# Decoder on one core: the first tile's running sums ahead of its last projection, row statistics elsewhere in the turn

## The chip, the core and the metric

The kernel runs on one core of one Trainium2 chip. The core has five engines with a queue of instructions each: TensorE (PE) multiplies matrices into eight PSUM banks, VectorE (DVE), ScalarE (ACT) and GpSimd (POOL) work elementwise, and SyncE (SP) only issues DMAs. Each queue runs in its own order; the engines meet at semaphores. The metric is device time in microseconds (us) of one execution. Before the change it is 1161.15 us, the median of three runs (1160.86 to 1164.18).

## The reference

The input is 4 sequences of 512 rows with 512 numbers each, seen as 16 tiles of 128 rows. Six blocks follow one another: a state-space mixer, a read from a memory, a routed feed-forward block, a grouped attention, a second memory read in fp8, and a feed-forward block with rounded weights. The change touches the mixer alone, `mamba3_forward` on `_layernorm(x)`:

```python
u_n = layer_norm(u, ln_w, ln_b)
proj = jnp.einsum('bsd,ed->bse', u_n, in_proj_w)   # z 1024, x 1024, B 128, C 128, dt 16
B = rms_norm(B, bnorm_w);  C = rms_norm(C, cnorm_w)
dA = softplus(dt + dt_bias) * -jnp.exp(A_log)
y = ssd_chunked(x, dA, B, C, CHUNK)   # pairs within a chunk decay by exp(differences of running sums of dA),
                                      # earlier chunks come in through a state
y = y + x * D[None, None, :, None]
y = y * jax.nn.silu(z_flat)
return u + jnp.einsum('bse,de->bsd', y, out_proj_w)
```

## The kernel before

The mixer works tile by tile, with chunks of 128 rows. The order is written out by hand, once for each engine (`tensor_program`, `vector_program`, `scalar_program`, `gpsimd_program`). A prologue takes tile 0 through its projections. Then a loop over i = 1 to 17, called turns here, overlaps three tiles: tile i is projected ("new"), tile m = i-1 gets its decays, products and gate ("mix"), and tile k = i-2 is turned, multiplied by the output weights and added to x ("old"). Four tiles are a sequence; its last hands on no state.

What the change and the prediction speak of, with the lines of `before`:

- **Running sums.** `decay_logs(i)` on POOL (L2063 to L2076) makes the logarithms of tile i's decays and lays them out in the tile `cum`; `running(i)` on PE (L455) sums them down the rows with one matmul; `high_cum` on ACT (L1608) and `low_cum` on DVE (L891) split the sums in a high and a low half; `shape_cum` on ACT (L1618, L1622) puts signs on them; four `spread_cum` on DVE (L901) spread them over heads into `cum_h`. `decay(m, q)` on PE (L469) multiplies these, for tile m in turn m+1, `exp_decay` on ACT (L1632) takes the exponential, `weigh_pair` on DVE (L909) multiplies it with the pair products.
- **Gate.** `project(i, 3)` and `project(i, 4)` on PE (L403) make z; `tanh_z(i, n)` on ACT (L1594) and `gate_z(i, n)` on DVE (L942) turn it into its gate; `gate_y(m, n)` on DVE (L934, L937) uses it.
- **Skip term.** `skip_y(m)` on POOL (L2115) writes x times D into the tile `y`. In turn 1 it waits until `low_piece(5)` on DVE (L852) has taken a piece of the output weights, since `y` lies where a later piece lands. `weigh_xs(m)` (L2133) multiplies `xs` for the state once `y_product` (L488) is through; `state_product` (L499) waits for it.
- **Row statistics.** `a_stats(g)` on DVE (four L819, four L823) takes mean and variance of the four tiles of a sequence; `stats(g)` on POOL makes scales of them one turn later. It comes in turns 1, 5 and 9, for the tiles 4 to 7, 8 to 11 and 12 to 15. `normal(i+1)` on DVE (L831) opens turn i; `turn_un` on PE (L411), `scale_x` on ACT (L1551) and all later work of tile i+1 wait for it.
- **Banks.** `Banks.claim` hands out PSUM banks when the program is built, from a table of expected times and in the order of the claims; a claim waits until the bank's last content has been read.

## Time and profile before

| what | value |
|---|---|
| median of 3 runs | 1161.15 us |
| the profiled execution | 1161.08 us, its span 1159.4 us |
| PE, DVE, ACT, POOL busy | 1044.8, 855.3, 606.0, 464.5 us (90, 74, 52, 40% of the span) |
| chain that ended last | PE 48%, DVE 21%, POOL 14%, issue 9%, ACT 5%, DMA 1% |
| mean granted TensorE clock | 0.967 of full speed |

The span runs from the first to the last instruction of the profiled execution; 1.7 us lie around it. PE is busy for nine tenths of it, but a busy share is a mean: the mixer fills the first 470 us, and in its first 75 us PE stands idle several times. The chain that ended last is followed back from the last instruction, at each step to what released it; a shorter time must shorten this chain.

### The profile page before, as it was taken

To read this page: it belongs to the slowest core of one execution; us is meant where nothing else is said; L and a number is where in the kernel's file an instruction comes from. 1 tells how busy PE (TensorE), PEld (TensorE's weight loads), DVE (VectorE), ACT (ScalarE), POOL (GpSimd) and SP (SyncE) were. 2 spreads that over 40 slices of the span, in tenths; PEclk is the share of its full clock that TensorE was granted. 3 is DMA by queue.
4 is the path that set the end of the run, shared out by engine and by line. 5 is a ranking of instruction groups with operands and counts; after the bars stand their busy time and mean duration, and the time that the engine had idled before them with its cause. 6 is when DMAs were issued, how large, how long until landed. Compare 5 with 4: busy or idle time off the path is not lost.

```text
span 1159.4 us, 14674 instructions
## 1 busy us (share of the span) xinstructions
PE 1044.8 (90%) x4830; PEld 746.7 (64%) x4830; DVE 855.3 (74%) x1615; ACT 606.0 (52%) x1201; POOL 464.5 (40%) x727
## 2 busy tenths in 40 slices
PE   5789999999999999879999689997788999899796
PEld 3667887888778888644545377765556666666342
DVE  5677766776677666726776658776779999989974
ACT  4634444444434443135556547553457877777662
POOL 5344324332433233325778214113544544535420
PEclk9899999999999999989999889998889999999899
DMA  8200000000000000063010044500001112111123
GB/s 297 86 1 1 1 1 1 1 1 1 1 1 1 1 1 6 32 254 118 29 37 1 1 162 147 193 24 1 1 5 22 40 29 52 27 37 43 31 54 87
DMA packets 48427, 52.92 MB, mean 46 GB/s; under 512 B 34528, under 2 KB 35552, under 8 KB 46048
## 3 DMA queue, kind: packets, MB, share of 16 engines
q1 hardware_dynamic: 48352, 51.99, 14.0%
q8 instruction: 39, 0.64, 0.2%
q14 instruction: 36, 0.29, 0.1%
HBM read 39.92 MB, written 4.19 MB: 38 GB/s over the span
## 4 chain that ended last, share of the span: by engine, by line
PE 48%; DVE 21%; POOL 14%; issue 9%; ACT 5%; DMA 1%; DVEq 0%; POOLq 0%; ACTq 0%
PE bank L403 37%; PE bank L488 3%; PE bank L411 3%; DVE cum_h L901 2%; POOL pv L2323 2%; PE bank L479 1%; POOL wq L2239 1%; DVE at L1359 1%; DVE o L1389 1%; POOL wq L2243 1%; PE bank L469 1%; POOL wq L2249 1%; DVE fm L1472 1%; DVE half_lo L1235 1%; POOL wq L2232 1%
## 5 line engine op out<-in xcount | busy, mean ns | idle before, releaser
L403 PE MATMUL bank<-win_hi,a_uT_hi 128*128 128x512 f32 (+1 forms) x320 | 130.1, 407 | 7.3 <-DVE win_lo L852 4.0
L403 PE MATMUL bank<-win_lo,a_uT_hi 128*128 128x512 f32 (+1 forms) x320 | 122.3, 382 | 0.0
L403 PE MATMUL bank<-win_hi,a_uT_lo 128*128 128x512 f32 (+1 forms) x320 | 122.0, 381 | 0.0
L2125 POOL TENSOR_TENSOR y<-y,off 128x512 f32<-128x512 f32 x24 | 37.8, 1573 | 113.8 <-DVE off L922 113.8
L1603 ACT ACTIVATE ex<-bank 128x48 f32<-128x48 f32 x16 | 3.3, 209 | 150.8 <-PE bank L447 150.8
L403 PEld LDWEIGHTS bank<-win_hi,a_uT_hi 128*128 128x128 f32 x320 | 62.5, 195 | 22.0 <-issue 6.4
L403 PEld LDWEIGHTS bank<-win_lo,a_uT_hi 128*128 128x128 f32 x320 | 62.6, 196 | 13.4 <-issue 2.9
L403 PEld LDWEIGHTS bank<-win_hi,a_uT_lo 128*128 128x128 f32 x320 | 62.1, 194 | 11.9
L403 PE MATMUL bank<-wq,eT 128*128 128x512 f32 x128 | 63.5, 643 | 4.9 <-ACT eT L1897 4.6
L488 PEld LDWEIGHTS bank<-xs,wgt 128*128 128x128 f32 x512 | 61.2, 192 | 6.8 <-issue 5.7
L403 PE MATMUL bank<-f,fqT_next 128*128 128x512 fp8e4 (+1 forms) x312 | 64.0, 362 | 1.3 <-DMA fqT_next<-fq 1.3
L488 PE MATMUL bank<-xs,wgt 128*128 128x64 f32 x512 | 61.0, 272 | 0.4 <-DVE wgt L909 0.4
L909 DVE SCALAR_TENSOR_TENSOR wgt<-wgt,cb 128x512 f32<-128x512 f32 x64 | 54.1, 845 | 8.6 <-ACT wgt L1632 8.4
L403 PE MATMUL bank<-wq,b_uT 128*128 128x512 f32 x128 | 59.7, 611 | 0.7 <-issue 0.7
L901 DVE TENSOR_TENSOR cum_h<-cum,eye_h 64x512 fp32r<-64x512 f32 x64 | 59.6, 970 | 1.0 <-ACT cum L1622 0.5
L403 PE MATMUL bank<-ctx,pT 128*128 128x512 f32 x128 | 58.2, 598 | 0.0
L1594 ACT ACTIVATE zs<-bank 128x512 f32<-128x512 f32 x32 | 18.8, 588 | 67.8 <-PE bank L403 67.8
L2050 POOL TENSOR_SCALAR sq<-sq 128x2 f32<-128x2 f32 x16 | 3.1, 191 | 127.2 <-ACT cs L1568 127.1
L403 PE MATMUL bank<-wout_hi,yT_hi 128*128 128x512 f32 x128 | 51.9, 406 | 1.6 <-DVE yT_lo L974 1.6
L403 PEld LDWEIGHTS bank<-f,fqT_next 128*128 128x128 bf16 x312 | 29.6, 98 | 34.6 <-issue 4.5
L403 PE MATMUL bank<-wout_lo,yT_hi 128*128 128x512 f32 x128 | 50.5, 394 | 0.0
L403 PE MATMUL bank<-wout_hi,yT_lo 128*128 128x512 f32 x128 | 50.4, 394 | 0.0
(335 smaller groups left out, 3046.1 us busy)
## 6 DMA issues: line engine op xcount, KB each, us to landing
wchunk<-w_in SPq DMA_DIRECT2D x32, 256.0 KB, 5.0
stage<-f_in SPq DMA_DIRECT2D x4, 1408.0 KB, 5.9
x<-x_in SPq DMA_DIRECT2D x16, 256.0 KB, 6.0
land<-win_in SPq DMA_DIRECT2D x4, 1024.0 KB, 7.6
wq<-ctxT_in SPq DMA_DIRECT2D x4, 1024.0 KB, 8.3
ctx<-ctx_in SPq DMA_DIRECT2D x4, 1024.0 KB, 5.7
out<-x SPq DMA_DIRECT2D x16, 256.0 KB, 2.7
first_stage<-f_in SPq DMA_DIRECT2D x2, 1408.0 KB, 14.2
```

What stands on the lines that cost most here:

```text
L403: made = e.matmul(bank, a, b, start=start and n == 0, stop=stop and n == len(pairs) - 1)
L411: made = e.transpose(bank[:, k * P:(k + 1) * P], src[:, k * P:(k + 1) * P], idn[:])
L469: e.matmul(bank[:], cum_s[q // 2][rows, :], cum_h[q][rows].rearrange("p a b -> p (a b)"), start=True, stop=True).then_inc(sig("decay_summe ...
L479: e.matmul(bank[:], cT[:], state[:, n * 512:(n + 1) * 512], start=True, stop=True).then_inc(sig("off_done"), 1)
L488: made = e.matmul(bank[:, j * HD:(j + 1) * HD], wgt[h // HG][:, h % HG, :], xs[m % 2][:, h * HD:(h + 1) * HD], start=True, stop=True)
L901: e.tensor_tensor(cum_h[q][rows], cum[rows, :].bitcast(F32).unsqueeze(1).broadcast_to([P // 2, HG, P]), eye_h[rows, first:first + HG].unsq ...
L909: e.scalar_tensor_tensor(out=wgt[q][:], in0=wgt[q][:], scalar=1.0, in1=cb[:].unsqueeze(1).broadcast_to([P, HG, P]), op0=ALU.min, op1=ALU.m ...
L1235: e.tensor_tensor(half_lo[m][f % 2][:], wchunk[m][f % WCHUNKS][:], half_hi[m][f % 2][:].bitcast(F32), ALU.subtract).then_inc(sig(f"half_lo ...
L1359: e.tensor_reduce(raw, prod[:, 0:s + 1, :].rearrange("p t (h d) -> p (t h) d", d=AHD), AX.X, ALU.add).then_inc(sig("at_step"), 1)
L1594: e.activation(zs[i % 2][:, n * 512:(n + 1) * 512], banks.of["proj_z", i, 3 + n][:], ACT.Tanh, scale=0.5).then_inc(sig("z_tanh"), 1)
L2125: e.tensor_tensor(y[m % 2][:, cols], y[m % 2][:, cols], off[:], ALU.add).then_inc(sig("y_off"), 1)
L2323: e.tensor_tensor(grouped(pv[turn % 2][:]), shared(n - n % BATCH + t, (R + 1) * AHD), weights(n, t), ALU.mult).then_inc(sig("pv_ready"), 1)
```

## The change

Nothing is computed otherwise. Four edits move work:

1. On PE, `running(0)` comes ahead of `project(0, 4)`. On ACT, `high_cum(0)` and `shape_cum(0)` come ahead of the tile's two or one last steps (`tanh_z(0, 0)`, `tanh_z(0, 1)`, `scale_x(1)`).
2. On DVE, `low_cum(0)` comes ahead of `gate_z(0, 0)`, the four spreads of tile 0 move from turn 1 into the prologue, and `gate_z(0, 1)` from the prologue into turn 1, behind `turned_bc(0)`.
3. On POOL, in turn 1 alone, `skip_y(0)` comes behind `decay_logs(1)`.
4. On DVE, `a_stats` moves in turns 1, 5 and 9 from behind the last two spreads to ahead of `gate_z(i, 1)`.

```diff
@@ tensor_program
             turn_un(1)
+            running(0)
             project(0, 4)
-            running(0)
@@ vector_program
             e.tensor_tensor(bcw[:], bw[:], cw[:], ALU.mult).then_inc(sig("mixer_consts"), 1)
+            low_cum(0)
             gate_z(0, 0)
-            gate_z(0, 1)
-            low_cum(0)
+            for q in range(NG):
+                spread_cum(0, q)
@@ vector_program, in the loop
                 if mix:
                     turned_bc(m)
                 if i == 1:
-                    for q in range(NG):
-                        spread_cum(0, q)
+                    gate_z(0, 1)
@@
                 if old:
                     low_yT(k, 1)
+                if i + 3 < NT and (i + 3) % TPB == 0:
+                    a_stats((i + 3) // TPB + 1)
                 if new:
                     gate_z(i, 1)
@@
                 if new:
                     spread_cum(i, 2)
                     spread_cum(i, 3)
-                if i + 3 < NT and (i + 3) % TPB == 0:
-                    a_stats((i + 3) // TPB + 1)
@@ scalar_program
             scale_x(0)
+            high_cum(0)
             tanh_z(0, 0)
+            shape_cum(0)
             tanh_z(0, 1)
             scale_x(1)
-            high_cum(0)
-            shape_cum(0)
@@ gpsimd_program
                     root_bc(i)
-                if mix:
+                if mix and i > 1:
                     skip_y(m)
                 if new:
                     decay_logs(i)
+                if i == 1:
+                    skip_y(m)
```

VectorE at the end of the prologue and the start of turn 1, - before and + now (`zs` is the gate, `un` the normalised tile, `cb` and `cT` the turned B and C):

```order
-L942 SCALAR_TENSOR_TENSOR zs_111<-zs_111,bank 128x512 x2
-L891 TENSOR_TENSOR cum<-bank,cum 32x128 x2
+L891 TENSOR_TENSOR cum<-bank,cum 32x128 x2
+L942 SCALAR_TENSOR_TENSOR zs_111<-zs_111,bank 128x512
+L901 TENSOR_TENSOR cum_h_115<-cum,eye_h 64x512
+L901 TENSOR_TENSOR cum_h_116<-cum,eye_h 64x512
+L901 TENSOR_TENSOR cum_h_117<-cum,eye_h 64x512
+L901 TENSOR_TENSOR cum_h_118<-cum,eye_h 64x512
 L831 TENSOR_SCALAR un<-x_51,a_mv_88,a_rs_90 128x512
 L878 COPY cb<-bank 128x128
 L880 TENSOR_SCALAR cT<-bank,bcw 128x128
```

The low half and the four spreads now stand ahead of the normalisation of tile 2, and one of the two gate steps stands behind `cT`, where the spreads had been.

VectorE at the end of turn 5, before the change (`yT_lo` and `y` belong to the tiles k and m, `a_st` and `a_mv` are the statistics of the next rows):

```order
L974 TENSOR_TENSOR yT_lo<-bank,yT_hi 128x512
L942 SCALAR_TENSOR_TENSOR zs_112<-zs_112,bank 128x512
L901 TENSOR_TENSOR cum_h_115<-cum,eye_h 64x512
L901 TENSOR_TENSOR cum_h_116<-cum,eye_h 64x512
L934 TENSOR_TENSOR y_123<-y_123,bank 128x512
L937 TENSOR_TENSOR y_123<-y_123,zs_111 128x512
L901 TENSOR_TENSOR cum_h_117<-cum,eye_h 64x512
L901 TENSOR_TENSOR cum_h_118<-cum,eye_h 64x512
L819 BN_STATS a_st<-x_57 128x6
...
L823 BN_AGGR a_mv_88<-a_st 128x2 x4
L980 SCALAR_TENSOR_TENSOR x_52,b_sum<-bank,x_52 128x512
```

The same place in the changed kernel:

```order
L974 TENSOR_TENSOR yT_lo<-bank,yT_hi 128x512
L819 BN_STATS a_st<-x_57 128x6
...
L823 BN_AGGR a_mv_88<-a_st 128x2 x4
L942 SCALAR_TENSOR_TENSOR zs_112<-zs_112,bank 128x512
L901 TENSOR_TENSOR cum_h_115<-cum,eye_h 64x512
L901 TENSOR_TENSOR cum_h_116<-cum,eye_h 64x512
L934 TENSOR_TENSOR y_123<-y_123,bank 128x512
L937 TENSOR_TENSOR y_123<-y_123,zs_111 128x512
L901 TENSOR_TENSOR cum_h_117<-cum,eye_h 64x512
L901 TENSOR_TENSOR cum_h_118<-cum,eye_h 64x512
L980 SCALAR_TENSOR_TENSOR x_52,b_sum<-bank,x_52 128x512
```

The eight statistics instructions stand ahead of the gate step instead of ahead of the addition to x; turns 1 and 9 read alike.

GpSimd in turn 1, before (`sq` are the norms of B and C, `dt` the logarithms of tile 1):

```order
L2050 TENSOR_SCALAR sq_101<-sq_101 128x2
L2052 TENSOR_TENSOR sq_101<-sq_101,mhalf 128x2
L2115 TENSOR_TENSOR y_123<-xs_109,dvec 128x1024
L2063 TENSOR_SCALAR dt_103<-dt_103 128x16
L2065 TENSOR_TENSOR dt_103<-dt_103 128x16
L2068 TENSOR_TENSOR dt_103<-dt_103,nega 128x16
L2070 CAST cum<-dt_103 128x4x8
L2072 TENSOR_TENSOR cum<-dt_103,cum 128x4x8
L2076 TENSOR_SCALAR cum<-cum 128x8x8
L2133 TENSOR_TENSOR xs_109<-xs_109,ex_113 128x1024
```

Now L2115 stands behind L2076 and ahead of L2133; nothing else moves there.

## Rows read from the trace of the kernel before

**Rows 1.** Granted clock by stretches: busy us and counts of the engines, PEclk, DMA share, GB/s.

```profile
31.30:36.00 4.70, 4.67 (x11) 3.70 (x12) 2.16 (x3) 1.53 (x2) 2.61 (x4) 0.50 0.86 318
42.80:46.20 3.40, 3.40 (x9) 2.59 (x9) 1.43 (x7) 3.10 (x11) 0.92 (x2) 0.51 0.01 2
190.00:192.00 2.00, 2.00 (x10) 1.90 (x9) 0.17 (x1) 1.71 (x9) 0.70 (x2) 0.50 0.04 8
```

**Rows 2.** Instructions of PE in order of time: start, us, what, [idle before, releaser].

```profile
31.33 0.80 PE L403 MATMUL bank<-win_hi,a_uT_hi 128*128 128x512 f32 x1 [4.02 <-DVE win_lo L852]
...
38.58 0.38 PE L447 MATMUL bank<-dt,ones 128*128 128x16 f32 x2
41.16 0.48 PE L469 MATMUL bank<-cum_h,cum_s 67*128 67x512 f32 x1 [2.21 <-DVE cum_h L901]
...
57.95 0.30 PE L455 MATMUL bank<-upto_r,cum 128*128 128x128 f32 x1 [3.13 <-POOL cum L2076]
...
66.57 3.57 PE L499 MATMUL bank<-xs,bs 128*128 128x512 f32 x4 [3.73 <-POOL xs L2133]
...
74.91 0.63 PE L411 MATMUL bank<-ident,un 128*128 128x128 f32 x4 [2.07 <-DVE un L831]
```

**Rows 3.** ACT in order of time, end of the prologue.

```profile
38.78 0.99 ACT L1618 ACTIVATE cum_s<-cum,signs 64x128 fp32r<-64x128 f32 x2 [0.74 <-DVE cum L891]
...
40.20 0.19 ACT L1603 ACTIVATE ex<-bank 128x48 f32<-128x48 f32 x1
```

**Rows 4.** POOL in order of time, prologue and turn 1.

```profile
28.89 0.25 POOL L2076 TENSOR_SCALAR cum<-cum 128x64 fp32r<-128x64 f32 x1
...
30.42 3.68 POOL L2105 CAST cum_h<-off 3x512 fp32r<-3x512 f32 x4
...
52.91 2.22 POOL L2115 TENSOR_TENSOR y<-xs,dvec 128x1024 f32<-128x1024 f32 x1 [7.86 <-DVE wout_lo L852]
...
57.56 0.25 POOL L2076 TENSOR_SCALAR cum<-cum 128x64 fp32r<-128x64 f32 x1
63.02 3.40 POOL L2133 TENSOR_TENSOR xs<-xs,ex 128x1024 f32<-128x1024 f32 x1 [5.22 <-PE bank L488]
```

**Rows 5.** DVE in order of time, turns 1 and 2.

```profile
40.33 2.61 DVE L901 TENSOR_TENSOR cum_h<-cum,eye_h 64x512 fp32r<-64x512 f32 x4 [0.51 <-ACT cum L1622]
...
58.60 0.59 DVE L891 TENSOR_TENSOR cum<-bank,cum 32x128 fp32r<-32x128 f32 x2 [0.26 <-ACT cum L1608]
61.78 0.69 DVE L942 SCALAR_TENSOR_TENSOR zs<-zs,bank 128x512 f32<-128x512 f32 x1 [2.59 <-ACT zs L1594]
...
64.59 2.98 DVE L901 TENSOR_TENSOR cum_h<-cum,eye_h 64x512 fp32r<-64x512 f32 x2
...
68.93 1.29 DVE L901 TENSOR_TENSOR cum_h<-cum,eye_h 64x512 fp32r<-64x512 f32 x2
70.25 2.47 DVE L819 BATCH_NORM_STATS2 a_st<-x 128x6 f32<-128x512 f32 x4
...
73.05 1.26 DVE L969 COPY state<-bank 128x512 f32<-128x512 f32 x2
74.23 0.54 DVE L831 TENSOR_SCALAR un<-x,a_mv,a_rs 128x512 f32<-128x512 f32 x1
```

**Rows 6.** DVE in order of time, turns 5 and 6.

```profile
178.02 0.69 DVE L942 SCALAR_TENSOR_TENSOR zs<-zs,bank 128x512 f32<-128x512 f32 x1 [1.35 <-ACT zs L1594]
178.63 2.85 DVE L901 TENSOR_TENSOR cum_h<-cum,eye_h 64x512 fp32r<-64x512 f32 x2
...
188.75 0.54 DVE L831 TENSOR_SCALAR un<-x,a_mv,a_rs 128x512 f32<-128x512 f32 x1
```

**Rows 7.** PE in order of time, starts of turns 6, 10 and 11.

```profile
189.43 0.90 PE L411 MATMUL bank<-ident,un 128*128 128x128 f32 x4 [1.20 <-DVE un L831]
...
304.06 0.63 PE L411 MATMUL bank<-ident,un 128*128 128x128 f32 x4 [1.20 <-DVE un L831]
...
334.26 0.63 PE L411 MATMUL bank<-ident,un 128*128 128x128 f32 x4 [0.82 <-DVE un L831]
```

## The prediction

> **What bounds the kernel now.** I read the chain that ended last first. Between 37 and 75 us it hardly touches PE: it goes over the split and shaping of tile 0's running sums, ACT's exponentials, `skip_y(0)` and `decay_logs(1)` on POOL, one projection on PE, then DVE's whole tail of turn 1 with `a_stats` in it. From turn 3 on it is mostly PE, except at the ends of the turns 5 and 9, where it goes through `a_stats` again. The instructions of PE in order of time give the holes: 4.02 us before `project(0, 4)`, 2.21 us before `decay(0, 0)` behind the spreads, 3.13 us before `running(1)` behind `decay_logs(1)`, 3.73 us before the state product behind `weigh_xs(0)`, and 2.07 us before tile 3's turning behind `normal(3)` [rows 2]; later 1.20 us in each of turns 6 and 10, and 0.82 us in turn 11 [rows 7]. All these lie in the mixer, whose first turn fills slowly. The blocks behind it start when its last tiles are through and their loads wait for those too, so I let every us gained in the mixer pass to the end.
>
> I follow one chain, from tile 0's sums to `normal(3)`, and then the two later places. In front of each step I ask which of its waits ends last.
>
> **Edit 1 and 2, the first tile's sums.** `running(0)` needs `decay_logs(0)`, which ends at 28.89 + 0.25 = 29.14 us [rows 4]. PE is idle until 31.33 [rows 2], so the matmul of some 0.3 us costs nothing there; the margin before it would hold up `project(0, 4)`, now queued behind it, is 2.2 us. The split follows on ACT and DVE, which both wait for `project(0, 4)` in that time. What ends last for `shape_cum(0)` is not the split but POOL's constant rows in `cum_h`, at 30.42 + 3.68 = 34.10 [rows 4]. The shaping takes from 38.78 to DVE's start at 40.33, 1.55 us [rows 3, 5]: the spreads start near 35.7 and end 2.61 us later at 38.3, where they ended at 42.94 before.
>
> That is 4.6 us on the spreads, but the next steps have other waits. `decay(0, 0)` goes right behind the sums, which end at 38.96 [rows 2], so 2.2 us earlier. ACT's exponential of the sums started at 40.20 because it queued behind the shaping [rows 3]; now it waits for the same 38.96 and starts at 39.0. From there ACT works through `scale_x(2)`, two pieces of output weights, two table loads and `exp_decay(0, 1)` with no idle that matters, so this chain gains only 40.20 - 39.00 = **1.2 us**. `normal(2)` is ready at 38.9 and hides in it. The gate step moved into turn 1 costs 0.69 us of DVE [rows 5] between `cT` and the wait for ACT's squares, which is longer. The second projection of turn 1 has its bank from this gate, and starts about 1 us behind `decay(0, 0)` as before, so 2 us earlier. It ends long before `weigh_pair(0, 1)`, which is what `y_product` waits for. So PE gets its time back and uses it for waiting.
>
> **Edit 3, POOL.** `skip_y(0)` started at 52.91, 7.86 us idle behind a weight piece, and `decay_logs(1)` behind it ended at 57.81; `running(1)` waited 3.13 us [rows 4, 2]. Now `decay_logs(1)` runs as soon as ACT's logarithm is there, inside those 7.86 us, and `running(1)` goes right behind `decay(0, 3)`, around 53.5. `skip_y(0)` still waits for the piece (at 52.7 - 1.2 = 51.5) and is still ready for the first `gate_y`. The 4.4 us gained on PE do not reach the end as such: DVE takes `low_cum(1)` only when the weighing and gating before it are through, which had started at 58.60 after 0.26 us idle [rows 5]. It now starts at 58.60 - 1.2 - 0.26 = 57.15. But the second `y_product` is no longer behind a late projection: it follows the last weighing (57.15), ends near 58.1, and `weigh_xs(0)` starts at 58.2 instead of 63.02.
>
> **Edit 4 in turn 1.** `low_cum(1)` ends at 57.75, and DVE used to wait 2.59 us from there for the tanh [rows 5]. `a_stats(2)` takes 73.05 - 70.25 = 2.80 us [rows 5] and fills it: the gate step starts at 60.55 instead of 61.78, still 1.2 us early. Then two things go. The first pair of spreads took 2.98 us and the second, the same work, 1.29 [rows 5]; the first ran against `weigh_xs(0)`, itself 3.40 us long (63.02 to 66.42), because the two excluded each other [rows 4, 5]. With `weigh_xs(0)` at 58.2 to 60.1 they don't meet: **1.7 us**. And `a_stats` is gone from the tail: **2.8 us**. `normal(3)` starts at 74.23 - 1.2 - 1.7 - 2.8 = 68.5; the state product, at 60 to 64, and everything else it needs are there. Start: **-5.7 us**.
>
> `a_stats` itself now runs beside `weigh_xs(0)`. No row shows such a pair. From below its cost is 0; from above one excludes the other, by the 1.7 us of the nearest rows (L901 against L2133). I take 0: of the DVE rows beside long POOL ones, those with one input in SBUF kept their length, those with two did not. The Trainium skill, "SBUF — State Buffer", section Who interferes with whom, says that a DVE instruction with at most one SBUF input and outside the two-port modes does not contend with GpSimd, and one with two does against a GpSimd read. By that rule the cost is 0 too; the first pair of spreads, two inputs, agrees.
>
> Turn 2 keeps its shape behind `normal(3)`: squares, norms, `skip_y(1)`, `stats(2)` and `add_off` on POOL set its pace, each as long as before. PE may run slower there (see the third rival); its slack I estimate at 2 us, 0.8 from the wait that comes a turn later (as in turn 11 [rows 7]) and 1.2 from POOL's chain being the later one of the two that `low_cum(2)` waits for,.
>
> **Edit 4 in turns 5 and 9.** DVE stood idle 1.35 us before the gate step at 178.02 [rows 6]. `a_stats` starts there at 176.67 and ends at 179.47, so gate and spreads begin 1.45 us later. The spreads took 2.85 us against `weigh_xs(4)`, which ends at 180.3; now they begin at 180.1 and take about 1.5. So `gate_y(4, 1)` is 0.1 to 0.3 us late, and the tail without `a_stats` puts `normal(7)` at 188.75 - 2.8 + 0.3 = 186.3. PE wants it at 189.43 - 1.20 = 188.2 [rows 7]: the whole wait of 1.20 us goes, and 1.1 us of the gain lies idle. ACT's `scale_x(7)` and `exp_decay(5, 0)` follow the sums instead of `normal(7)`, 1.2 to 1.3 us earlier, and with them POOL's `stats(3)` chain, the later gates and `normal(8)`. In turn 6 PE also ran at the lower level of the clock, 1.2 GHz, for a while (0.50 in 190 to 192 us [rows 1]), in turn 10 not. Getting that back does not count: turn 10 shows what binds next, 0.82 us of waiting for `normal` in turn 11 [rows 7]. Per place 1.3 us, from 0 (all of it waited away in the next turn) to 2.9 (turn 6's wait and its slow stretch). Two places: **-2.6 us**.
>
> **Sum.** -5.7 - 2.6 = -8.3 us on 1161.08, the profiled execution, which stands 0.07 us from the median: 1152.8. Bank choices shift in the mixer by a swap of tile 0's two last claims; each later claim of turns 2 to 5 waits for the same thing as before, so I give them 0, within half a us. I round to **1153**.
>
> **Rivals.**
>
> *Gains waited away, 1156.* If `a_stats` and `weigh_xs` exclude each other, the start loses 1.8 of its 5.7 us; if the holes of turns 6 and 10 only move to turns 7 and 11 (0.82 us stands there already), the places give nothing. Either alone gives 1155, both 1157. For it: the rows show that each stall here hides another. Against: ACT and POOL chains start earlier too, not only PE. Chance 0.2.
>
> *No change, 1160.* Something behind the mixer does not move with it. For it: blocks behind it are paced by loads. Against: the loads wait for mixer events, DMA is 1% of the chain. Or turn 1 is paced by ACT all through, which would leave only 1.2 us. Against: of the time from 58.60 to 74.23 DVE waited for ACT 2.85 us and worked through the rest [rows 5]. Chance 0.08.
>
> *Slower, 1165: the clock.* Each longer hole of PE can put it at 1.2 GHz: after 4.02 us idle the clock was at 0.50 for 4.7 us, after 2.21 at 0.51 for 3.4 us, after 1.20 at 0.50 in turn 6 [rows 1, 2, 7], and after the 1.20 of turn 10 not. A stretch costs half its length, 1.7 to 2.35 us. The new order concentrates PE's waiting: about 3.5 us before `y_product(0, 0)` and 4 us before `normal(3)`, besides the waits in turns 3, 7 and 11. It decides from the point where PE is late for DVE: beyond the 2 us of slack in turn 2, 0.8 in the later turns. If all five fell for 4.7 us and PE's next work were all bound by it, 12 us come back, on 1153. Against: four of five have slack. Chance 0.03.
>
> The Trainium skill, "TensorE: Matmul & The Clock Gate", section Part 1: The HAM clock gate, says that idleness throttles the array to half rate and activity releases it. The falls above agree in kind; the turn 10 row shows a hole of the same length without one.
>
> **How the numbers follow.** My forecast has 0.66, with 1151 to 1155 as its own range; a further 0.03 I leave to more than 10 us, if slow stretches of turns 1 and 6 vanish as well. The range for 8 in 10 reaches from 1150 to 1157.5 and takes in the first rival. This kernel tells 0.3%, 3.5 us, from no change: below 1157.7 is faster. That is the forecast, the upper end and nearly all of the first rival: 0.87; the same 0.10; slower 0.03.
>
> **What would show it.** `running(1)` near 53.5 us without wait for POOL; `weigh_xs(0)` near 58, 1.9 us long; the four L819 beside it still 2.47 us; the first spreads of turn 1 at 1.3 us; `normal(3)` near 68.5; no wait for `normal` in turns 6 and 10, and at most 0.8 to 1.5 us in 7 and 11; the mixer's end 8 us earlier. Wrong would be a `normal(3)` after 71, a stretch at 1.2 GHz in turn 3, 7 or 11 that the next waits don't swallow, or a start of the second block that has not moved by what turn 11 has.

## The result, and the profile after

The changed kernel takes 1152.59 us (median of six runs, 1151.33 to 1154.3) beside 1161.91 of the kernel before, measured with it (1160.86 to 1165.31): a ratio of 0.9914, 95% interval 0.9897 to 0.993, 9.3 us less. The forecast was 1153. The profiled execution took 1152.76 us, its span is 1151.0.

Further down the changed kernel is measured a second time: 0.9945, interval 0.9929 to 0.9961, 1153.3 beside 1160.62, 7.3 us between the medians. The two intervals just touch at 0.993. The second pair fits better to what the change gives in the mixer, as the experiments show. Its traced execution is the slowest of its six (1157.57 us, mean granted clock 0.964 for 0.972 in three of the others), so its trace shows the change at its worst.

Up to `normal(3)` the chain came as worked out. VectorE, end of the prologue and turn 1 of the changed kernel, in order of time (start, us, what, [idle before, releaser]):

```profile
35.63 2.61 DVE L901 TENSOR_TENSOR cum_h<-cum,eye_h 64x512 fp32r<-64x512 f32 x4 [1.62 <-ACT cum L1622]
...
56.88 0.59 DVE L891 TENSOR_TENSOR cum<-bank,cum 32x128 fp32r<-32x128 f32 x2
57.51 2.47 DVE L819 BATCH_NORM_STATS2 a_st<-x 128x6 f32<-128x512 f32 x4
60.01 0.38 DVE L823 BATCH_NORM_AGGREGATE a_mv<-a_st 128x2 f32<-128x6 f32 x4
60.42 0.69 DVE L942 SCALAR_TENSOR_TENSOR zs<-zs,bank 128x512 f32<-128x512 f32 x1
61.03 2.28 DVE L852 TENSOR_TENSOR wout_lo<-land,wout_hi 128x2048 fp32r<-128x2048 f32 x1
63.23 1.28 DVE L901 TENSOR_TENSOR cum_h<-cum,eye_h 64x512 fp32r<-64x512 f32 x2
...
65.86 1.29 DVE L901 TENSOR_TENSOR cum_h<-cum,eye_h 64x512 fp32r<-64x512 f32 x2
67.19 1.29 DVE L969 COPY state<-bank 128x512 f32<-128x512 f32 x2
68.51 0.55 DVE L831 TENSOR_SCALAR un<-x,a_mv,a_rs 128x512 f32<-128x512 f32 x1
```

They answer to [rows 5]: the idle of 2.59 us is filled by the statistics, the first pair of spreads is as long as the second, and `normal(3)` starts at 68.51 in place of 74.23. GpSimd in the same time:

```profile
46.83 0.25 POOL L2076 TENSOR_SCALAR cum<-cum 128x64 fp32r<-128x64 f32 x1
51.49 2.21 POOL L2115 TENSOR_TENSOR y<-xs,dvec 128x1024 f32<-128x1024 f32 x1 [4.41 <-DVE wout_lo L852]
58.19 1.90 POOL L2133 TENSOR_TENSOR xs<-xs,ex 128x1024 f32<-128x1024 f32 x1 [4.48 <-PE bank L488]
```

`decay_logs(1)` ends at 47.1, 10.7 us earlier than in [rows 4], and `weigh_xs(0)` is 1.90 us long and lies wholly beside the statistics (58.19 to 60.09 within 57.51 to 60.39). PE, the places of [rows 2] and [rows 7]:

```profile
53.21 0.22 PE L455 MATMUL bank<-upto_r,cum 128*128 128x128 f32 x1
...
60.23 2.50 PE L499 MATMUL bank<-xs,bs 128*128 128x512 f32 x4 [2.22 <-POOL xs L2133]
...
69.21 1.09 PE L411 MATMUL bank<-ident,un 128*128 128x128 f32 x4 [2.81 <-DVE un L831]
...
85.23 0.22 PE L455 MATMUL bank<-upto_r,cum 128*128 128x128 f32 x1
...
100.71 0.63 PE L411 MATMUL bank<-ident,un 128*128 128x128 f32 x4
...
183.69 0.60 PE L411 MATMUL bank<-ident,un 128*128 128x128 f32 x4
...
214.06 0.63 PE L411 MATMUL bank<-ident,un 128*128 128x128 f32 x4 [0.81 <-DVE un L831]
...
297.03 0.60 PE L411 MATMUL bank<-ident,un 128*128 128x128 f32 x4
...
327.41 0.63 PE L411 MATMUL bank<-ident,un 128*128 128x128 f32 x4 [0.81 <-DVE un L831]
```

The waits of 1.20 us in the turns 6 and 10 are gone, 0.81 us stands in turn 7 and 11. The one in turn 7 does not come from the change: it stands as well in the three kernels below that keep the statistics of turn 5 in the old place and whose clock did not fall in turn 6, and is missing in the two whose clock fell there. VectorE in turn 5 of the changed kernel, which answers to [rows 6]:

```profile
172.19 2.46 DVE L819 BATCH_NORM_STATS2 a_st<-x 128x6 f32<-128x512 f32 x4
174.69 0.38 DVE L823 BATCH_NORM_AGGREGATE a_mv<-a_st 128x2 f32<-128x6 f32 x4
174.99 0.66 DVE L942 SCALAR_TENSOR_TENSOR zs<-zs,bank 128x512 f32<-128x512 f32 x1
175.56 1.53 DVE L901 TENSOR_TENSOR cum_h<-cum,eye_h 64x512 fp32r<-64x512 f32 x2
...
181.85 0.54 DVE L831 TENSOR_SCALAR un<-x,a_mv,a_rs 128x512 f32<-128x512 f32 x1
```

One thing was not in the sum. Granted clock (third column from the right) of the changed kernel in stretches of turns 1 and 2:

```profile
62.00:66.00 4.00, 4.00 (x22) 3.48 (x21) 3.94 (x6) 0.00 (x0) 0.00 (x0) 0.63 0.00 0
66.00:70.00 4.00, 1.19 (x6) 0.90 (x6) 3.45 (x7) 1.11 (x3) 0.00 (x0) 0.79 0.00 0
70.00:74.00 4.00, 4.00 (x15) 3.42 (x14) 2.14 (x8) 3.68 (x10) 2.84 (x4) 0.50 0.02 4
74.00:80.00 6.00, 6.00 (x24) 4.46 (x23) 1.41 (x3) 3.06 (x6) 5.11 (x12) 0.90 0.00 0
```

Behind the hole of 2.81 us before tile 3's turning PE ran at 1.2 GHz until some 75 us. `normal(3)` was 5.7 us ahead, but `running(2)` behind it, at 85.23, only 3.0 (before 88.26). By tile 4's turning, 100.71 in place of 105.15, 4.4 us are left: 1.3 us of the start are lost. The slow stretch in 62 to 66 us is an earlier one, behind the hole of 2.22 us before the state product; `normal(3)` came at 68.51 all the same.

This table follows the gain through all kernels of this study. "Tile 4" is the start of tile 4's turning, at the start of turn 3. "Mixer" is the start of the load of the second block's weights `wq`, 461.86 us in the profile of before; it is a mark in one profiled execution each.

| kernel | median us (before, measured with it) | ratio, 95% interval | normal(3) | tile 4 | mixer |
|---|---|---|---|---|---|
| before | 1161.15 | | 74.23 | 105.15 | 461.86 |
| changed | 1152.59 (1161.91) | 0.9914, 0.9897 to 0.993 | 68.51 | 100.71 | 455.04 |
| changed, second time | 1153.3 (1160.62) | 0.9945, 0.9929 to 0.9961 | 70.84 | 101.76 | 456.05 |
| edits 1, 2 | 1159.78 (1160.41) | 0.9989, 0.9975 to 1.0002 | 73.28 | 104.20 | 460.84 |
| edits 1, 2, 3 | 1159.9 (1160.41) | 0.9985, 0.9971 to 0.9999 | 71.80 | 103.39 | 460.11 |
| edit 3 | 1157.53 (1160.19) | 0.9976, 0.9964 to 0.9989 | 70.92 | 102.19 | 458.75 |
| edit 4 | 1157.7 (1160.41) | 0.9974, 0.9957 to 0.9991 | 71.26 | 102.59 | 456.77 |
| changed, edit 4 in turn 1 only | 1157.94 (1160.41) | 0.9965, 0.995 to 0.9981 | 69.78 | 100.83 | 457.68 |
| changed, two holds | 1154.19 (1160.62) | 0.9941, 0.9927 to 0.9955 | 69.46 | 100.41 | 454.76 |
| changed, three holds | 1152.69 (1160.19) | 0.993, 0.9916 to 0.9943 | 68.71 | 99.78 | 454.03 |
| changed, stats late | 1148.58 (1160.62) | 0.9902, 0.9886 to 0.9917 | 68.65 | 99.74 | 450.57 |
| stats late, four holds | 1146.91 (1160.62) | 0.9882, 0.9867 to 0.9896 | 70.73 | 100.25 | 451.22 |
| stats late, five holds | 1144.0 (1160.19) | 0.9858, 0.9845 to 0.9872 | 68.83 | 98.33 | 449.11 |

From the mixer's mark to the end of the span it is 697.5 us in before and 696.0, 699.8, 694.5, 696.3, 696.1, 695.2, 699.9, 698.1, 696.1, 694.8, 693.9 and 693.5 us in the others, in the order of the table. No edit but the last holds touches that part, so single executions differ there by some 3 us either way, and a gain of the mixer is better read at its mark than at the end. The traced execution is not a typical one either: those of edits 1, 2 and of edit 4 are the fastest of their twelve, those of the changed kernel's second time and of edit 4 in turn 1 only the slowest of theirs.

Between tile 4's turning and the mark the kernels agree far better. It is 356.6 to 356.9 us in the five with the statistics of turns 5 and 9 in the old place, 354.2 to 354.4 in the five that have edit 4 there, and 350.8 to 351.0 in the three with stats late. So edit 4 in these two turns gives 2.4 us in every kernel, and stats late 3.5 more; all other differences at the mark arise ahead of tile 4's turning.

### The profile page after: what moved, and what is told of

Read it like the earlier page. It is cut to its first block, busy times and chain, and to the rows that moved or that the text cites. A ratio compares the mean times of both kernels' runs of the same rounds, so it can differ in the third digit from the quotient of the medians.

```text
span 1151.0 us, 14674 instructions
## 1 busy us (share of the span) xinstructions
PE 1040.8 (90%) x4830; PEld 746.2 (65%) x4830; DVE 852.1 (74%) x1615; ACT 605.9 (53%) x1201; POOL 462.2 (40%) x727
## 4 chain that ended last, share of the span: by engine, by line
PE 50%; DVE 19%; POOL 14%; issue 9%; ACT 5%; DMA 1%; DVEq 0%; POOLq 0%; ACTq 0%
PE bank L403 38%; PE bank L488 4%; PE bank L411 3%; POOL pv L2325 2%; PE bank L479 1%; DVE cum_h L901 1%; POOL wq L2241 1%; DVE at L1359 1%; PE bank L499 1%; DVE o L1389 1%; PE bank L469 1%; POOL wq L2245 1%; POOL wq L2251 1%; DVE fm L1472 1%; DVE half_lo L1235 1%
## 5 line engine op out<-in xcount | busy, mean ns | idle before, releaser
L2125 POOL TENSOR_TENSOR y<-y,off 128x512 f32<-128x512 f32 x24 | 38.0, 1585 | 116.4 <-DVE off L922 116.4
L403 PEld LDWEIGHTS bank<-win_lo,a_uT_hi 128*128 128x128 f32 x320 | 62.5, 195 | 13.2 <-issue 2.9
L403 PE MATMUL bank<-wq,eT 128*128 128x512 f32 x128 | 60.7, 618 | 4.9 <-ACT eT L1897 4.6
L403 PE MATMUL bank<-ctx,pT 128*128 128x512 f32 x128 | 58.2, 598 | 0.0
L901 DVE TENSOR_TENSOR cum_h<-cum,eye_h 64x512 fp32r<-64x512 f32 x64 | 55.3, 902 | 2.1 <-ACT cum L1622 1.6
```

Source lines behind the costliest of these rows:

```text
L403: made = e.matmul(bank, a, b, start=start and n == 0, stop=stop and n == len(pairs) - 1)
L901: e.tensor_tensor(cum_h[q][rows], cum[rows, :].bitcast(F32).unsqueeze(1).broadcast_to([P // 2, HG, P]), eye_h[rows, first:first + HG].unsq ...
L2125: e.tensor_tensor(y[m % 2][:, cols], y[m % 2][:, cols], off[:], ALU.add).then_inc(sig("y_off"), 1)
```

## The experiments

**The first tile's sums alone (edits 1 and 2).**

```diff
+            running(0)
             project(0, 4)
-            running(0)
@@ vector_program: low_cum(0) ahead of both gates, spreads in the prologue, gate_z(0, 1) in turn 1
@@ scalar_program: high_cum(0), shape_cum(0) ahead of tanh_z and scale_x(1)
```

> The kernel before with edits 1 and 2 alone (first tile's sums and spreads earlier on all engines), nothing else. Theory (one chain, ACT's exponentials then DVE): scale_x(2) and all of turn 1 come 1.2 to 1.4 us earlier and nothing else changes, since running(1) still waits for skip_y(0) and decay_logs(1); normal(3) near 72.9 us instead of 74.23, time -1.4 us, ratio 0.9988. Rival (what PE stops waiting for counts): PE's hole of 2.2 us before decay(0, 0) and its slow clock behind it go, -3.5 us, ratio 0.997.

`normal(3)` moved by 0.95 us and the mixer's mark by 1.0, near the forecast 1.2; the time itself can't be told from no change. The spreads start 4.5 us earlier (35.83 in place of 40.33), and of that only 1.0 us arrives, near ACT's 1.2.

**Edits 1, 2 and 3.**

```diff
-                if mix:
+                if mix and i > 1:
                     skip_y(m)
                 if new:
                     decay_logs(i)
+                if i == 1:
+                    skip_y(m)
```

> Edits 1, 2 and 3 (skip_y(0) behind decay_logs(1)), statistics where they were. Theory: low_cum(1) starts 1.7 us earlier, weigh_xs(0) no longer meets the spreads (pair of L901 1.3 instead of 2.98 us), so normal(3) at 74.2 - 1.7 - 1.7 = 70.8 us, -3.4 us at that point, less up to 1.5 us if TensorE falls to 1.2 GHz in turn 2; time -2 to -3.4 us, ratio 0.997 to 0.998. Rival (edit 3 gives PE its 3.13 us and all of it counts): -4.5 to -6 us, ratio 0.995 to 0.996.

`normal(3)` at 71.80, a us later than expected, and the mark only 1.75 us earlier; the medians are 0.5 us apart, where 2 to 3.4 were expected. Granted clock by stretches, then VectorE and GpSimd of this kernel:

```profile
50.00:54.00 4.00, 4.00 (x15) 3.34 (x15) 4.00 (x3) 0.52 (x2) 2.21 (x1) 0.60 0.00 0
```

```profile
60.28 3.67 DVE L852 TENSOR_TENSOR wout_lo<-land,wout_hi 128x2048 fp32r<-128x2048 f32 x1
63.87 1.28 DVE L901 TENSOR_TENSOR cum_h<-cum,eye_h 64x512 fp32r<-64x512 f32 x2
```

```profile
59.90 1.90 POOL L2133 TENSOR_TENSOR xs<-xs,ex 128x1024 f32<-128x1024 f32 x1 [6.06 <-PE bank L488]
```

PE had waited 1.63 us inside the first `y_product` and then ran at 1.2 GHz, so the second `y_product` and `weigh_xs(0)` came 1.7 us late. The spreads are free of it, but the piece of weights ahead of them, `low_piece(6)` (L852), met it and took 3.67 us where it takes 2.28. The collision moved, by way of the clock. Behind `normal(3)` another 0.7 us is lost by tile 4's turning (103.39), with a second slow stretch behind a hole of 5.95 us before tile 3's turning (0.53 in 70 to 74 us).

**Edit 3 alone.** The diff is the one above, on the kernel before.

> Edit 3 alone: skip_y(0) behind decay_logs(1), all else as before. Theory (the collisions go by where weigh_xs(0) lies): running(1) some 4 us earlier, but DVE takes low_cum(1) only when its weighing is through, so -0.26 there; weigh_xs(0) comes to about 59.5 and the first spreads of turn 1 take 1.3 us in place of 2.98, if low_piece(6) is not met instead. normal(3) near 72.3 (-2.0), the mixer's end -1.0 to -2.0, time 1158.5 to 1159.7 beside 1160.5 of before. Rival 1 (PE's late running(1) itself set the pace of turn 1): normal(3) near 71.0 and -3.1 or more at the mixer's end. Rival 2 (edit 3 needs edit 1 to have any effect): nothing, normal(3) 74.2.

The numbers came out as the first rival had them (70.92, -3.3; the mark -3.1; the medians -2.7), but mostly by the theory's way:

```profile
49.09 0.69 DVE L909 SCALAR_TENSOR_TENSOR wgt<-wgt,cb 128x512 f32<-128x512 f32 x1 [2.11 <-ACT wgt L1632]
...
57.52 0.59 DVE L891 TENSOR_TENSOR cum<-bank,cum 32x128 fp32r<-32x128 f32 x2
60.18 0.69 DVE L942 SCALAR_TENSOR_TENSOR zs<-zs,bank 128x512 f32<-128x512 f32 x1 [2.07 <-ACT zs L1594]
60.79 2.28 DVE L852 TENSOR_TENSOR wout_lo<-land,wout_hi 128x2048 fp32r<-128x2048 f32 x1
62.99 1.28 DVE L901 TENSOR_TENSOR cum_h<-cum,eye_h 64x512 fp32r<-64x512 f32 x2
```

`running(1)` is some 4 us earlier, yet `low_cum(1)` only 1.1, and 0.8 of these were there at 49.09 already (before 49.87), where edit 3 has done nothing yet: PE's clock was 0.72 in 31 to 37 us here and 0.58 in the profile of before. So 0.8 from the first hole's clock, 0.3 from the wait for ACT, 0.5 from a shorter wait for the tanh, 1.7 from the collision: 3.3. Here the clock was 1.00 in 50 to 54 us, `weigh_xs(0)` lay at 58.83 to 60.73 and passed both its neighbours.

**The statistics alone (edit 4, all three turns).**

```diff
                 if old:
                     low_yT(k, 1)
+                if i + 3 < NT and (i + 3) % TPB == 0:
+                    a_stats((i + 3) // TPB + 1)
                 if new:
                     gate_z(i, 1)
...
-                if i + 3 < NT and (i + 3) % TPB == 0:
-                    a_stats((i + 3) // TPB + 1)
```

> Edit 4 alone (a_stats ahead of gate_z(i, 1) in turns 1, 5 and 9). Theory: in turn 1 the tail loses 2.8 us and the gate step comes 0.2 us later, weigh_xs(0) still meets low_piece(6) and the spreads: normal(3) near 71.6 us, -2.6; turns 5 and 9 give 1.3 us each; time -4 to -5.2 us, ratio 0.9955 to 0.9965. Rival (the holes only move to the next turns): -2.6 us in turn 1 and nothing later, ratio 0.9978.

`normal(3)` at 71.26 and the mark 5.1 us earlier: by the traces this edit is most of the gain. The medians are 2.7 us apart, less than the 4 to 5.2 expected; the trace is that of the fastest execution. Of the 3.0 us of `normal(3)`, 0.7 stand ahead of the statistics (`low_cum(1)` at 57.92 in place of 58.60, again with a clock of 0.72 in 31 to 37 us), so its own part there is 2.3 us, and 4.4 at the mark. The gate step could start 0.3 us earlier than before (61.46), the spreads behind it still took 2.99 us beside `weigh_xs(0)`.

**The changed kernel with edit 4 in turn 1 only.**

```diff
-                if i + 3 < NT and (i + 3) % TPB == 0:
+                if i == 1:
                     a_stats((i + 3) // TPB + 1)
...
+                if i in (5, 9):
+                    a_stats((i + 3) // TPB + 1)
```

> The changed kernel, but a_stats in turns 5 and 9 behind the spreads as before. Theory: the 1.20 us waits of turns 6 and 10 return, with 0.8 us in turn 11: 2.5 us slower than the changed kernel, that is 1155.1 on a median of 1152.6, ratio to before 0.9935. Rival (those two places give nothing): as fast as the changed kernel, ratio 0.9914. In the profile normal(3) stays at 68.5 us.

The waits of 1.20 us stand again in the turns 6 and 10. The mark is at 457.68, 2.6 us behind the changed kernel's first profile and 1.6 behind its second, but these differ ahead of tile 4. From tile 4's turning to the mark it is 356.85 us, as in the kernel before (356.71), beside 354.33 and 354.29 in the changed kernel: the places of turns 5 and 9 give 2.5 us here, 2.6 by the forecast. The ratio came out as 0.9965, not the 0.9935 expected: that was reckoned from the first pair's 0.9914, and from the second's 0.9945 it is 0.2% off, about these 2.5 us. `normal(3)` did not stay at 68.5 but came at 69.78; the reason is given further down.

**The changed kernel a second time.** No edit.

> The changed kernel once more, beside variants of it on one chip. Single executions of one kernel spread by 2 to 4 us, so the first pair of medians (1161.91 and 1152.59, ratio 0.9914) may hold some luck. Theory (the mixer alone gains, 6.8 us in the first trace, and the blocks behind it gain nothing): ratio 0.994. Rival (all 8.4 us of the first trace are the change's): ratio 0.992 or less.

The same code took another way through the start. `normal(3)` comes at 70.84, tile 4's turning at 101.76 with a wait of 0.81, the mark at 456.05:

```profile
50.00:54.00 4.00, 4.00 (x14) 3.42 (x15) 4.00 (x3) 0.70 (x2) 2.20 (x1) 0.50 0.00 0
...
70.00:74.00 4.00, 2.46 (x16) 2.24 (x17) 1.99 (x6) 2.28 (x9) 0.59 (x2) 1.00 0.02 4
```

```profile
57.21 0.69 DVE L942 SCALAR_TENSOR_TENSOR zs<-zs,bank 128x512 f32<-128x512 f32 x1 [1.25 <-ACT zs L1594]
...
62.69 2.96 DVE L852 TENSOR_TENSOR wout_lo<-land,wout_hi 128x2048 fp32r<-128x2048 f32 x1
```

Here the clock fell in turn 1 and not in turn 2. The slow projection of z made VectorE wait 1.25 us for the tanh, where it had not waited in the first profile, and the late `weigh_xs(0)` (61.60) stretched `low_piece(6)` to 2.96 us. Of the 2.3 us by which `normal(3)` is later than in the first profile, 1.65 stand at `low_cum(1)` (58.53 in place of 56.88) and 0.7 come from the collision.

**Two holds.** Products that nobody reads, from the identity into a bank that the next real product overwrites: 18 before the first state product, 24 before tile 3's turning.

```diff
+            def keep_busy(bank, times):
+                for _ in range(times):
+                    e.transpose(bank[:, 0:P], ident[:], ident[:])
...
+                if i == 3:
+                    keep_busy(bank, 24)
                 w.wait_ge("u_ready", i + 1)
...
+                    if m == 0 and n == 0:
+                        keep_busy(bank, 18)
                     w.wait_ge("xs_weighted", si + 1)
```

> The changed kernel plus 42 matmuls (turnings of the unit matrix into a bank just claimed, not read) in two holes of PE, 18 before the first state product and 24 before tile 3's turning, so that PE isn't idle there. Theory (the hole lets TensorE fall to 1.2 GHz in turn 2, and this ate 1.3 us of the forecast's 5.7): running(2) near 82.7 us instead of 85.2, tile 4's turning near 99.4 instead of 100.7, 1.3 us faster than the changed kernel. Rival (turn 2 is paced by something else): running(2) earlier or not, tile 4's turning stays at 100.7 and the time too.

The clock was 1.00 from 62 to 80 us, and from `normal(3)` (69.46) to tile 4's turning (100.41) it is 30.95 us, in place of 32.20 in the first profile: the 1.3 us of the theory. But it is 30.92 in the second profile too, whose clock had not fallen there, and in the kernel before. So the mark at 454.76, 1.3 us ahead of the second profile, is no gain of these holds; it comes from `normal(3)`, 1.4 us ahead. The time is not told apart (0.9941 beside 0.9945). `normal(3)` was late by 1.0 us against 68.5: 0.5 stood at the first `y_product` already, and 0.5 came from `low_piece(6)` (2.76 us), since the clock fell in 50 to 54 us (0.59), ahead of the first hold.

**Three holds.** Another 13 such products in the hole inside the first `y_product`:

```diff
+                    if m == 0 and n == 0 and j == HG:
+                        for _ in range(13):
+                            e.transpose(bank[:, 256:256 + P], ident[:], ident[:])
                     w.wait_ge("w_ready", NG * m + h // HG + 1)
```

> The changed kernel with products that nobody reads in three holes of PE: 13 in the wait inside the first y_product, 18 before the first state product, 24 before tile 3 is turned. Theory (the clock's fall at 50 us, seen in some executions of the changed kernel and not in others, makes running(1) and with it weigh_xs(0) late, until it meets low_piece(6)): clock 1.00 in all stretches from 48 to 80 us, running(1) 53.2 to 53.7, weigh_xs(0) near 58.4 and 1.9 long, low_piece(6) under 2.3, normal(3) 68.5 to 68.8, tile 4's turning near 99.5, the mixer's end near 454.0 (before 461.9), time 0.5 to 1.5 us under that of the version with two holds. Rival (VectorE sets turn 1's pace whatever PE's clock is): normal(3) at 69.4 as with two holds and no difference in time.

```profile
50.00:54.00 4.00, 4.00 (x22) 3.35 (x22) 4.00 (x3) 1.22 (x4) 2.21 (x1) 1.00 0.00 0
...
70.00:74.00 4.00, 4.00 (x15) 3.27 (x16) 1.94 (x8) 3.68 (x11) 2.72 (x3) 0.60 0.00 0
```

```profile
53.40 0.22 PE L461 MATMUL bank<-upto_r,cum 128*128 128x128 f32 x1
...
69.31 0.66 PE L411 MATMUL bank<-ident,un 128*128 128x128 f32 x4 [1.74 <-DVE un L842]
```

(The added lines shift the numbers: L461 is L455.) `running(1)` at 53.40, `weigh_xs(0)` at 58.38, `low_piece(6)` 2.28 long, `normal(3)` at 68.71, tile 4's turning at 99.78, the mark at 454.03, 0.7 us ahead of the two holds: the theory, against the rival's 69.4. Of these 0.7 us 0.3 stood ahead of the hold, at the first `y_product` (46.69 for 46.97). One part failed: the second filler ran out and 1.74 us of hole were left behind it, after which the clock stood at 0.60 in 70 to 74 us. In time it is 1.5 us under two holds by the medians (1152.69, 1154.19), on different chips, with intervals that overlap.

**GpSimd's statistics later.** In the changed kernel VectorE waited 3.42 us in turn 6 for the sum `y` (L2125), which stood on GpSimd behind the ten instructions of `stats(3)`:

```profile
191.43 0.19 POOL L2029 TENSOR_SCALAR a_rs<-a_mv 128x4 f32<-128x4 f32 x1
...
196.48 1.28 POOL L2125 TENSOR_TENSOR y<-y,off 128x512 f32<-128x512 f32 x1
```

```profile
197.79 0.69 DVE L934 TENSOR_TENSOR y<-y,bank 128x512 f32<-128x512 f32 x1 [3.42 <-POOL y L2125]
```

```diff
-                if i + 2 < NT and (i + 2) % TPB == 0:
-                    stats((i + 2) // TPB + 1)
                 if mix:
                     add_off(m, 0)
+                if i + 2 < NT and (i + 2) % TPB == 0:
+                    stats((i + 2) // TPB + 1)
+                if mix:
                     add_off(m, 1)
```

> The changed kernel with the scales of the next rows (stats on POOL, turns 2, 6 and 10) between the two add_off instead of ahead of both. Theory (after the change the wait that takes the place of the old one is DVE's for POOL's add_off behind stats, which leaves 0.8 us for normal and 0.5 us for weigh_xs in turns 7 and 11): both waits go, 1.3 us for each of two places, 2.6 us faster than the changed kernel. Rival (stats there delays add_off(m, 1) and weigh_xs, so the state product waits instead): same or up to 2 us slower.

1148.58 us, 4.7 under the changed kernel's second time by the medians, and the mark 5.5 us earlier than there, where 2.6 were expected. But `normal(3)` was 2.2 us earlier already, ahead of the place where this edit first works, and tile 4's turning 2.0: this trace had the better start. The edit's own part is the 3.5 us behind tile 4, the same against the first profile. The same places now, GpSimd and VectorE:

```profile
192.35 1.59 POOL L2125 TENSOR_TENSOR y<-y,off 128x512 f32<-128x512 f32 x1 [1.98 <-DVE off L922]
194.02 0.52 POOL L2029 TENSOR_SCALAR a_rs<-a_mv 128x4 f32<-128x4 f32 x1
```

```profile
194.41 0.67 DVE L934 TENSOR_TENSOR y<-y,bank 128x512 f32<-128x512 f32 x1
```

The wait is gone; so are the 0.81 us in turns 7 and 11 (tile 8's turning at 211.40 without a wait, in place of 214.06). From tile 4's turning to tile 8's it is 111.66 us, 1.7 less than in the changed kernel (113.35).

**Stats late with four and with five holds.** The four: 18 and 24 as above, 26 before the last tile's pair product and 40 before the second block's first turning. The five: the 13 of turn 1 as well.

```diff
+                if m == NT - 1:
+                    keep_busy(bank, 26)
                 w.wait_ge("bcT_ready", m + 1)
...
+                if i == 0:
+                    keep_busy(bank, 40)
                 w.wait_ge("u_ready", NT + i + 1)
```

> e7 and e6 together, and the same filling matmuls in two more holes of PE, 26 before the last pair product in turn 16 (3.05 us idle) and 40 before the first turning of the second block (5.0 us idle). Theory: 1.3 + 2.6 us as there, and 1 to 1.5 us each where PE ran at 1.2 GHz behind the two later holes: 5 to 7 us faster than the changed kernel. Rival (work behind those holes is paced by DVE, ACT and DMA, not by PE): no more than e6 and e7 together, 4 us.

1146.91 us, on the chip of the kernel without holds (1148.58); that is 6.4 us under the changed kernel, in the range of the theory, but the intervals of this ratio and of stats late alone overlap, so what the holds add is not shown by the times. The mark did not move forward (451.22 beside 450.57), again with 0.50 in 50 to 54 us: `normal(3)` was 2.1 us later, tile 4's turning only 0.5, with the clock held at 1.00 in turn 2.

> All three holds, POOL's stats between the two add_off, and products that nobody reads before the last tile's pair product (26) and the second block's first turning (40). Theory: the gains add: normal(3) 68.5, tile 4's turning without wait near 98.8, the mixer's end 449.5 to 450.5, time 1145.3 to 1147.0. Rival (the next wait, POOL or VectorE, swallows the hold of turn 1): the mixer's end 451.2 and 1146.9 as without it.

1144.0 us, ratio 0.9858, the best of all: the mark at 449.11 and tile 4's turning at 98.33, a little ahead of the theory, with a clock of 1.00 in every stretch from 37 to 80 us. Against four holds tile 4's turning gains 1.9 us and the mark 2.1, the hold of turn 1: the first `y_product` starts at the same time in both (46.81 and 46.79). The intervals of the two ratios overlap a little, so in the time alone this is not told apart.

## Why the prediction was right, and what of it was not

The time (1152.59 for 1153) fell in the range and the direction was right, but the agreement to half a us is partly luck: the mixer gave 6.8 us in the first profile and 5.8 in the second, where the forecast had 8.3, and the medians lie 9.3 and 7.3 us apart. The other 1.6 us between the two spans of the first pair (8.4) lie behind the mixer, where executions differ by that much without any edit.

**Edits 1 and 2.** Right: the spreads started at 35.63 (35.7) and 1.0 us arrived when they were done alone, for 1.2.

**Edit 3.** Right: `running(1)` at 53.21 without a wait (53.5), `low_cum(1)` at 56.88 (57.15), `weigh_xs(0)` at 58.19 (58.2), the first spreads 1.28 us. Alone it gave 3.3 us at `normal(3)`, 2.5 without the first hole's clock; I had 2.0.

**Edit 4 in turn 1.** Right in place and price: the gate step at 60.42 (60.55), `normal(3)` at 68.51 (68.5). What statistics and `weigh_xs(0)` cost each other was open from 0 to 1.7 us; it is 0: 2.47 and 1.90 us, as long as each is alone. That rows with two inputs did not keep their length beside GpSimd was too much said: in the trace of before `low_piece(6)` kept its 2.28 us and `weigh_xs(0)`, which started behind it, took 3.40. By the rule in the Trainium skill, "SBUF — State Buffer", section Who interferes with whom, it would be 0; the trace agrees.

**The step that was mis-sized: "its slack I estimate at 2 us", and with it "Start: -5.7 us".** The start gave 4.4 us by tile 4's turning in the first profile, 3.4 in the second (101.76). In the first the loss of 1.3 us lies in turn 2, behind the hole of 2.81 us before tile 3's turning. From that turning to `running(2)` it is 13.2 to 13.4 us in the seven profiles whose clock was up there (13.35 in before), and 14.9 to 16.0 in the six with a slow stretch behind the hole, 16.02 in the changed kernel's first. So the stretch cost 2.7 us there, where I had at most 2.35. By tile 4's turning 1.4 us came back (15.48 us from `running(2)`, before 16.89), 0.81 of it the wait: the slack is 1.4 us, not 2.

The slack did not cover turn 1 at all: I had named the waiting before `y_product(0, 0)` in the third rival and then given it no price in the likeliest case. Of eight profiles with edits 1 and 2 and without the hold in turn 1, seven show a clock of 0.50 to 0.65 in 50 to 54 us; the eighth, with 1.00, is the changed kernel's first. The three kernels without edits 1 and 2 show 1.00 there and have their slow stretch in 42 to 47 us (0.66, 0.66, 0.72), where all that have these edits show 1.00: edits 1 and 2 move the fall from one place to the other. There it makes the second `y_product` late and with it `weigh_xs(0)`, until `low_piece(6)` meets it. In the five profiles that fell and have edit 4 in turn 1 the piece took 2.76 to 2.96 us. In the two of them at 0.50 VectorE also waited 1.2 us for the tanh. Counted from the first `y_product`, the fall costs `normal(3)` 1.9 to 2.0 us in these two and 0.5 in the other three (0.59 to 0.65). What else sets `normal(3)` off from 68.5, 0.4 us early to 0.8 late, stood at the first `y_product` already (46.10 to 47.27), 0.8 of it in the kernel with edit 4 in turn 1 only. With a hold there the start is as forecast in both kernels tried (68.71, 68.83). With all holds and stats late tile 4 is turned at 98.33, 6.8 us ahead of before. Of these some 1.4 are not the holds': with the clock held in turn 2 it is 16.92 us from `running(2)` to that turning, with a wait of 0.82, and 15.48 without it where GpSimd's statistics come later too.

This is also why the parts don't add. At the mixer's mark edits 1 and 2 alone give 1.0 us, edit 3 3.1, edit 4 5.1, 9.2 together, and the whole 5.8 to 6.8. Behind tile 4's turning they do add, since only edit 4 gives anything there, 2.4 to 2.5 us. Ahead of it they give 1.0, 3.0 and 2.6 us, and the whole 4.4 and 3.4. Of edit 3's and edit 4's parts 0.8 and 0.7 us are the faster first stretch of their profiles (0.72 for 0.58 in 31 to 37 us), which has nothing to do with the edits. Edit 3 is worth 3.1 alone but 0.7 on top of edits 1 and 2.

**Edit 4 in turns 5 and 9.** The mechanism was right: the gate step and spreads late by what the statistics take over the idle time, spreads of 1.53 us (1.5) in place of 2.85, the 1.20 us gone, 0.81 in the turns behind. Forecast 2.6 us, measured 2.4: from tile 4's turning to the mark 356.71 us in before, 354.33 and 354.29 in the changed kernel. The distance from tile 4's turning to tile 8's shrank by 219.79 - 105.15 - (214.06 - 100.71) = 1.3 us, and to tile 12's by another 1.1, for 1.3 each. It was right to count nothing for turn 6's slow stretch: the kernels that kept the wait of 1.20 us but not the slow stretch took 114.4 to 114.5 us from tile 4's turning to tile 8's, before 114.6.

**The rivals.** The first (gains waited away, 1156) was right in kind: part of the gain is waited away, in turns 7 and 11 and at VectorE's wait for `y`. It is smaller than that rival had it, and the wait has a place that it did not name, the statistics on GpSimd; taking it away gave 3.5 us in the mixer and 4.7 between the medians. The third (the clock) was right that the order draws PE's waiting together; it costs 1.3 us of the gain in the first profile and 2.0 in the second and does not reverse it. The clock fell in turns 1 and 2, and was 1.00 in the turns 3, 7 and 11 of both profiles. The second did not happen.

## What to carry to other kernels

Fill an engine's idle time in front of a wait with work that stands in its tail, and price such work by what it does to its new neighbours' collisions too: here that was 1.7 of the start's 5.7 us. When an edit makes an engine's front part earlier but leaves its next wait, the wait grows in one piece; for TensorE ask what the clock does behind it, and what an instruction that comes late will run against. When the first wait is gone, look for where VectorE now waits longest: moving GpSimd's row statistics by one place gave 3.5 us in the mixer, more than half of the whole change again. And read a gain between two marks of the same place in several kernels: kernels with the same edits there differed by 0.2 to 0.3 us, at the end of the span some 3.

## What the runs showed of the hardware

- TensorE's clock after a hole is not the same in every execution of one program. Behind the same 1.63 us hole (from 47.57 and from 47.87 us) the changed kernel ran at 2.4 GHz in one profile (granted 1.00 in 50 to 54 us) and at 1.2 GHz in the other (0.50). The chip of the first is not on record, so a difference between chips is not excluded. The Trainium skill, "TensorE: Matmul & The Clock Gate", section Part 1: The HAM clock gate, says that idleness throttles the array; the traces agree that slow stretches lie behind holes, and show that a hole does not always bring one.
- Products that nobody reads, in the hole, kept the clock at 1.00 behind it each time that they left less than 0.7 us of it open (13, 18, 24, about 0.12 us each); where 1.7 us were left open it fell once (0.60, behind 1.74 us) and once not (1.00, behind 1.72).
- Of a VectorE operation with both inputs in SBUF and a long GpSimd one with two, the one that starts second pays. Where `weigh_xs(0)` was ahead, `low_piece(6)` took 3.67 and 2.96 us for 2.28, and `weigh_xs(0)` its 1.90; where the piece was ahead (before, edits 1 and 2 alone, edit 4 alone) it kept its 2.28 or 2.29, `weigh_xs(0)` took 3.40 to 3.79, and the spreads behind it 2.98 or 2.99 for 1.28. The row statistics with one input lost nothing and cost nothing.
